# LSTM recurrence in rounds: low weights in pieces, another order between rounds, two-pass round with its rows in PSUM

## The reference

```python
x = x + gnn(layernorm(x), edge_index, W1, b1, W2, b2)     # segment sum over 100000 edges, two dense layers
x = x + ffn(layernorm(x)[None], W_f, b_f, ...)[0]
# ffn, for each of 6250 rows in order:
f_t = sigmoid(combined @ W_f + b_f); i_t = sigmoid(combined @ W_i + b_i)   # combined = (x_t, h_prev)
c_tilde = tanh(combined @ W_c + b_c)
c_t = f_t * c_prev + i_t * c_tilde
o_t = sigmoid(combined @ W_o + b_o)
h_t = o_t * tanh(c_t)
```

## Time and profile before

| | us |
|---|---|
| median of 3 runs | 2840.35 (2840.02 to 2848.08) |
| profiled execution | 2835.44 |
| its span, first to last instruction | 2833.9 |
| PE / DVE / ACT / POOL busy | 2506.7 / 2090.2 / 1585.3 / 1019.9 |

### The profile page before, as it was taken

How to read it: one execution, slowest core, us unless ns; L and a number is a source line. 1 busy time by engine, 2 the same in 40 slices (tenths; PEclk the granted TensorE clock), 3 DMA queues, 4 the chain that set the end, 5 groups by cost and what they waited for, 6 DMA issues and landing times.

```text
span 2833.9 us, 45183 instructions
## 1 busy us (share of the span) xinstructions
PE 2506.7 (88%) x10574; PEld 1840.8 (65%) x10575; DVE 2090.2 (74%) x5442; ACT 1585.3 (56%) x3682; POOL 1019.9 (36%) x1022
## 2 busy tenths in 40 slices
PE   6977999999999999998799988888887888788776
PEld 5765787788888778786566656666664555555444
DVE  5847888888888888887578766666666667666665
ACT  4644544454554444453267744444445888777775
POOL 0307777777777777776300000000000000033332
PEclk9998999999999999999899999999998999999998
DMA  8548988888898888887566557777776777689996
GB/s 238 154 137 249 281 265 259 250 272 271 269 280 270 253 254 265 249 265 227 171 166 185 147 168 237 235 234 231 236 237 170 212 204 213 187 233 260 270 266 188
DMA packets 209753, 648.73 MB, mean 229 GB/s; under 512 B 48762, under 2 KB 76794, under 8 KB 179954
## 3 DMA queue, kind: packets, MB, share of 16 engines
q1 hardware_dynamic: 136888, 410.93, 49.9%
q0 software_dynamic: 72816, 237.24, 28.3%
HBM read 493.87 MB, written 154.16 MB: 229 GB/s over the span
## 4 chain that ended last, share of the span: by engine, by line
PE 29%; DMA 6%; ACT 6%; DVE 6%; issue 2%; SPq 1%; DVEq 0%; ACTq 0%
PE acc L1506 24%; DMA xg<-total_rows 6%; PE hturn L1524 3%; ACT acc L1444 3%; ACT tc L1436 2%; ACT gate L1410 1%; DVE ic L1779 1%; PE acc L1532 1%; DVE total L1750 1%; DVE h L1792 1%; DVE c L1784 1%; DVE fc L1772 1%; DVE total L1752 1%; PE acc L1535 0%; DVE state L1766 0%
## 5 line engine op out<-in xcount | busy, mean ns | idle before, releaser
L1506 PE MATMUL acc<-W_high,state 128*125 128x512 f32 x2224 | 629.4, 417 | 71.6 <-ACT acc L1444 69.7
L1506 PEld LDWEIGHTS acc<-W_high,state 128*125 128x125 f32 x2224 | 410.4, 192 | 206.5 <-ACT acc L1444 88.2
L1359 POOL TENSOR_TENSOR out<-h,lx 125x512 f32<-125x512 f32 x50 | 64.3, 1286 | 1224.2 <-DVE h L1792 1224.2
L809 POOL DMA_INDIRECT rows<-ln_table,slab x400 | 400.7, 1002 | 249.5 <-issue 145.3
L809 POOL DMA_INDIRECT Wh<-ln_table,slab x400 | 430.4, 1076 | 121.9 <-issue 119.8
L910 PE MATMUL agg<-high,onehot 128*125 128x512 f32 x800 | 332.8, 416 | 29.7 <-DVE onehot L1007 18.5
L1506 PE MATMUL acc<-W_high,hT 128*125 128x512 f32 x784 | 325.1, 415 | 8.3 <-issue 0.2
L1020 DVE TENSOR_TENSOR low_part<-rows,high 128x512 fp32r<-128x512 f32 x400 | 254.1, 691 | 98.1 <-ACT high L866 83.5
L910 PE MATMUL agg<-low_part,onehot 128*125 128x512 f32 x800 | 322.0, 403 | 0.0
L1506 PE MATMUL acc<-W_low,hT 128*125 128x512 f32 x784 | 308.6, 394 | 0.0
L1772 DVE TENSOR_TENSOR fc<-gate,c 125x256 f32<-125x256 f32 x376 | 162.9, 433 | 188.6 <-ACT gate L1410 179.3
(11 more groups left out here) (211 smaller groups left out, 4483.1 us busy)
## 6 DMA issues: line engine op xcount, KB each, us to landing
xg<-total_rows SPq DMA_DIRECT2D x100, 896.0 KB
xg<-gate_rows SPq DMA_DIRECT2D x88, 896.0 KB
gate_rows<-gout SPq DMA_DIRECT2D x100, 448.0 KB
total_rows<-total SPq DMA_DIRECT2D x50, 896.0 KB
hT<-h_steps SPq DMA_DIRECT2D x98, 250.0 KB, 3.7
lx<-x_rows POOLq DMA_DIRECT2D x50, 250.0 KB, 8.6
out_dram<-out POOLq DMA_DIRECT2D x50, 250.0 KB, 8.7
h_steps<-hT SPq DMA_DIRECT2D x49, 250.0 KB, 3.2
```

Source lines behind the costliest of these rows:

```text
L809: e.indirect_dma_start(out=rows[j // 2][:, j % 2 * D:(j % 2 + 1) * D], out_offset=None, in_=table[:, :], in_offset=bass.IndirectOffsetOnAx ...
L1506: m = e.matmul(acc[n][0:L, :], stationary[:, k, :], weights[:, k, n // 2, n % 2].rearrange("p s c -> p (s c)"), start=begins, stop=(k == K ...
```

## The change

It edits `lstm_part` alone.

- Low weights: POOL makes them in 16 pieces of 512 columns, each behind the `decay` of a step of the rough round (the first behind that round's second step), and signals after every fourth.
- Near round: the rows of a step are copied into PSUM one step ahead (banks 0 and 3 by ACT, 1 and 2 by DVE), products add to them, gates are read from PSUM, and the sums are copied out to `total` (banks 0, 1, 2 by DVE, 3 by ACT) before the bank is seeded again. SP loads the rows of step s + 1 in step s. PE forms bank 3 of the first chunks after banks 0 and 1. At the first step PE adds the rows as fp32 products.
- Delta rounds: bank 0 gets its rows from PE (`add_rows(0)`), bank 3 from DVE, banks 1 and 2 from ACT as before.
- Between rounds: separate signals behind the transposes of `c`, of `decay` and of the gate; PE adds rows 0 and 1 before the start signal; the start signal comes after `state`, and a second one after `c`; what isn't needed for the start goes behind it. The near round's check is computed later: `h_gap` after the start of the delta round, its maxima in the measure and correct parts of the delta round, scaled by TOLERANCE / LOOSE, as two more columns of the last round's check.

```diff
@@ gpsimd @@
+            def low_weights():
+                for n in range(4 * K):
+                    k, half, bank = n // 4, n // 2 % 2, n % 2
...
+                    e.wait_ge(s_decay, AHEAD + LEFT_OUT + n + 2)
+                    piece = e.tensor_tensor(W_low[:, k, half, bank].rearrange("p s c -> p (s c)"),
...
@@ sync, near round @@
                     def keep(s, par, state_too):
-                        e.wait_ge(s_sum[3], f * STEPS + s + (AHEAD + 1))
+                        hold(e, s_passed, s_taken_out_v, s * 3 + 3)
+                        hold(e, s_passed, s_taken_out_a, s + 1)
                         spread(e, totals_v[s], total[par][0:L].rearrange("c a b g -> c (a b g)"), s_total_st[par])
...
@@ scalar @@
                     elif kind in DELTAS:
                         forget_input(1)
                         new_cell(FIRST)
                         cell_gate(1)
-                        seed(0)
                         seed(1)
                         output_gate(1)
                     elif kind == "near":
                         new_cell(FIRST)
+                        seed(0)
                         forget_input(1)
                         take_turned(FIRST, s, par, now)
                         cell_gate(1)
...
                     new_cell(SECOND)
                     if kind in DELTAS:
                         seed(2)
+                    elif kind == "near":
+                        take_out(3)
                         seed(3)
@@ tensor @@
                     def first_step():
-                        e.wait_ge(s_begin, r + 1)
-                        for n in range(4):
-                            m = add_rows(n)
-                        m.then_inc(s_taken, 1)
-                        for n in range(4):
+                        add_rows(0)
+                        add_rows(1)
+                        e.wait_ge(s_begin, r * 2 + 1)
+                        for n in range(2):
+                            for k in range(K):
+                                product(n, k)
+                        add_rows(2)
+                        e.wait_ge(s_begin, r * 2 + 2)
+                        add_rows(3).then_inc(s_taken, 1)
+                        for n in range(2, 4):
                             for k in range(K):
                                 product(n, k)
...
                     def delta_step():
+                        add_rows(0)
                         turn(FIRST, 1 - par, now - 1)
...
                     def near_step():
-                        for n in range(3):
-                            e.wait_ge(s_sum[n], summed - 1)
-                            products(n, FIRST, of_state, True)
+                        for n in range(2):
+                            seeded(n)
+                            add(n, FIRST)
+                        seeded(2)
+                        add(2, FIRST[:1])
                         if not first:
                             turn(SECOND, 1 - par, now - 1)
-                        e.wait_ge(s_sum[3], summed - 1)
-                        products(3, FIRST[:1], of_state, True)
+                        add(2, FIRST[1:])
                         for k in SECOND:
                             stated(k)
                         for n in range(2):
-                            products(n, SECOND, of_state, False).then_inc(s_acc[n], 1)
-                        products(3, FIRST[1:], of_state, False)
-                        products(2, SECOND, of_state, False).then_inc(s_acc[2], 1)
-                        products(3, SECOND[:1], of_state, False)
+                            add(n, SECOND).then_inc(s_acc[n], 1)
+                        seeded(3)
+                        add(3, FIRST).then_inc(s_taken, 1)
+                        add(2, SECOND).then_inc(s_acc[2], 1)
+                        add(3, SECOND[:1])
                         turn(FIRST, par, now)
@@ vector @@
+                    def take_out(n):
+                        half, bank = n // 2, n % 2
+                        e.wait_ge(s_total_st[par], (s - par) * (SPREAD // 2) + SPREAD)
+                        e.wait_ge(s_o[half] if bank else s_fi[half], now)
+                        e.tensor_copy(total[par][0:L, half, bank], acc[n][0:L, :]).then_inc(s_taken_out_v, 1)
+                    if kind == "near":
+                        forgotten(0)
+                        take_out(0)
+                        taken_in(0)
+                        for k in FIRST:
+                            new_cell(k)
+                        take_out(1)
+                        new_h(FIRST)
+                        seed(1)
+                        forgotten(1)
+                        take_out(2)
+                        seed(2)
+                        taken_in(1)
...
```

More of the change, by code:

```diff
@@ L1694, in measure @@
                 t.then_inc(s_ends, 1)
-                if kind not in ("rough", "delta"):
-                    e.wait_ge(s_worst, f + 1)
+                if kind in ("last", "more"):
+                    e.wait_ge(s_worst, f)
                     e.transpose(worst_t, worst[:, :], ident[:, :]).then_inc(s_worst_t, 1)
             def correct(r, kind):
+                if kind == "near":
+                    e.wait_ge(s_taken_out_a, STEPS)
                 e.wait_ge(s_cs, r + 1)
@@ L1825, in step @@
                             decayed()
-                        if kind == "rough" and not last:
-                            seed()
+                        seed(3)
                     else:
-                        if kind == "more" and not first:
+                        if not first:
                             low_part(SECOND, now - 1)
@@ L1851, in step @@
                         decayed()
-                        if kind == "more" and last:
+                        if last:
                             low_part(SECOND, now)
@@ L1885, in measure, with most_of @@
                     after_own(e.tensor_tensor(h_gap[:, k, 1:], hturn[k][:, 0:L - 1], h_start[:, k, 1:], ALU.subtract))
[L1886 to L1889 removed]
+            def most_of(n, g, op):
+                after_own(e.tensor_reduce(most[:, n:n + 1], g[:, :, :].rearrange("p k l -> p (k l)"), AX_X, op))
@@ new lines, in of_near_round, with measure @@
+            def of_near_round(n, op, sign):
+                most_of(n, h_gap, op)
+                after_own(e.tensor_scalar(most[:, n:n + 1], most[:, n:n + 1], sign * TOLERANCE / LOOSE, None, ALU.mult))
+            def measure(r, kind, f):
+                own[0] = own_before(r, kind)
+                signals[0] = 0
+                if kind == "delta":
+                    of_near_round(4, ALU.max, 1.0)
+                e.wait_ge(s_ends, r * 4 + 1)
+                after_own(e.tensor_tensor(gap[:, :, 1:], c_end_t[:, :, 0:L - 1], c_start[:, :, 1:], ALU.subtract))
+                if kind in ("rough", "near", "delta"):
+                    return
+                h_moved(r, kind)
+                for n, (g, op) in enumerate(((gap, ALU.max), (h_gap, ALU.max), (gap, ALU.min), (h_gap, ALU.min))):
+                    most_of(n, g, op)
@@ L1904, in correct @@
             def correct(r, kind):
+                e.wait_ge(s_ends, r * 4 + 2)
                 for k in range(K):
```

253 lines of the change are left out of this document (141 added, 112 removed).

## The result

The changed kernel takes 2816.97 us (median of 8 runs, 2802.63 to 2833.22) against 2841.59 for the kernel before (8 runs, 2838.65 to 2848.08): ratio 0.9916, 95% interval 0.9893 to 0.9939. The interval stands for 17 to 30 us less, so the times can't tell the 20 that I forecast from the 24.6 between the medians. I had forecast 2820, with a range of 2800 to 2833.

What follows compares the result with a forecast made beforehand. It took serial chains to bound the first three rounds and DMA bytes the last; terms -13.1 + 1.6 - 2 + 2.5 - 6.5 + 1 - 2.5 - 1 = -20 gave 2820 us, range 2800 to 2833.

Steps and rivals of the forecast that it cites:

- Start and pieces: Rough round: long POOL subtractions leave its start, -13.1 us; sixteen gated pieces cost +1.6 (bounds 0 and 7.8).
- The order of PE's first step: Start of rough round: PE forms banks 0 and 1 before adding rows 2 and 3, first gates earlier, -0.9 us.
- Rough to two-pass: Transition: `gap` 2.0 us earlier, cast and copy moved behind the start, fp32 additions added; -2 us (bounds 0 and -3.5).
- Two-pass steps: Additions leave the chain, copies and seeds join it; +0.05 us times 49, +2.5 (bounds -15 and +20).
- Two-pass to delta: Transition: check moved behind the start, rows added earlier, but row 0 lands late; -6.5 us (bounds -3 and -10).
- Delta steps: Delta round: PE's wait for ACT's seeds goes, transposes move 0.27 later, about cancelling; +1 us (bounds -3 and +7).
- Delta to last: Transition: products may begin earlier, but two additions stand among them; -2.5 us (bounds 0 and -4).
- Final check: End of kernel: `gap` earlier and one small operation less; -1 us.
- The forecast's case: Whole kernel: 2820 us, own range 2811 to 2830, chance 0.62.
- the start held back by late rows: Rival at the rough round's start: not freed because rows land late; 2824 us, counted inside the forecast's own range.
- The shorter two-pass step: Rival: both additions leave the chain and copies hide, -0.4 us a step, 2798 us; chance 0.15.
- the copies that take the chain: Rival in two-pass steps: copies and seeds lengthen the chain; +0.7 a step, 2852 us, chance 0.07; +0.4, 2837, chance 0.06.

Runs made afterwards that it cites:

- e1: Kernel before plus only the low weights in sixteen gated pieces on POOL, nothing else of the change; ratio 0.9962 to the kernel before, recurrence 1423.3 us against 1435.0.
- e6: Changed kernel with all sixteen pieces released after the first rough step instead of one a step; rough round 239.9 us against 225.9 in the changed kernel.
- e10: Changed kernel with 48 of the last round's 50 loads of x rows left out (output invalid); last stretch 322.2 us against 346.2.
- e4: Changed kernel with the two-pass round's seed of bank 2 moved from DVE to ACT; two-pass 466.1 us against 500.2, ratio 0.9805 to the kernel before.
- e7: Changed kernel with seed 2 and the copy out of bank 0 on ACT, delta row 0 loaded early; two-pass 456.3 us, ratio 0.9777 to the kernel before.
- e5: Changed kernel with the two-pass round's check put back ahead of the corrected state; turn-to-turn into delta 22.21 us against 22.87, recurrence 1411.6 us.
- e3: Changed kernel with the delta round's first row loaded in the last two-pass step, ahead of the stores; delta stretch 316.5 us against 324.0.

## Why the prediction was right, and where it was not

The sum was -20, the recurrence shows -21.5, and the medians -24.6, with the graph part's own variation in them. That the sum lies so near is in part luck: five terms missed by 2 to 3.4 us each, three one way and two the other, and the last stretch alone varies by 19 us from profile to profile. What held is where the gain would come from: the start and the places between rounds, and not the steps. Term by term:

- **Start and pieces, -13.1 + 1.6 = -11.5 forecast, -11.5 measured** (e1: -11.3). Its parts were off and cancelled. PE's start gave 1.8 and not 4.0. The two products held by the subtraction gave more than the 8.2 that I had: in e1, which has the pieces alone, the first gates of the first two steps stand 6.94 us apart, where it had been 15.66, -8.7, and the second step became 0.7 shorter too (5.65 for 6.32), which I had not counted. The order of PE's first step gave 0 and not 0.9 (above). The pieces cost 0 and not 1.6. For the start I had divided row 0's bytes by the whole bandwidth, while its load took 7.3 us with three more rows issued behind it. For the pieces, the rule in the Trainium skill, "SBUF — State Buffer", section "Who interferes with whom", which I had set beside the sum, was the better guide. By that rule in the Trainium skill, a copy with a single SBUF input outside the two-port modes doesn't hold a piece back. The trace agrees, with 0.69 and 1.29 side by side. That a product of two SBUF operands and a piece block each other whole is borne out by e6, with 1.52 for 0.42.
- **Rough to two-pass, -2 forecast, -4.3 measured** at the first gate (13.07 for 17.38). `gap`, and with it `c_start`, came 2.1 sooner as worked out, but the two additions took 2.2 us and lay beside the new states and the copy of `c`; I had them 3.1 long and on the path. The clock has a part in the rest: in e10, with the same code and a mean granted clock of 0.73 in place of 0.90, 2.6 of the 4.3 were left.
- **Two-pass steps, +2.5 forecast, -0.9 measured.** The balance held: what left the chain came back onto it. Two of its debits were measured by e4 and e7: 0.70 for the seed into bank 2 alone (I had 0.86 for it and the copy before it), 0.20 for the copy out of bank 0 (0.16). From the second `fc` to the second `h` it is 2.84 us, where it had been 1.52: 1.32 for those two copies, the whole 0.60 and 0.72 of my sum, with nothing of the 0.46 that I took off for a wait. So something else in the step gained more than I gave it; one such part is seen, the second transposes, which follow `h` by 0.35 us and not 0.79 (-0.44, I had -0.35). No run separates the rest, ACT's +0.42 among it, and that these errors cancelled is luck. The place where the time went is DVE's order in front of the second `ic`, as written; of PE's wait for `h` before its transposes, which I had left standing, 11.5 us of 49.2 are left.
- **Two-pass to delta, -6.5 forecast, -3.5 measured.** That PE would wait for the row was right, and its size was not: 6.68 us. I had the load issued at +5.2 us behind the last transposes (it was +5.5) and landed at +10.3 (it was +12.55), again by bytes over bandwidth plus one microsecond. The first product came 6.4 sooner, for 8. So -3.5 lay inside the bound of -3 only just. What I called DVE's gain was worth nothing there (e5).
- **Delta steps, +1 forecast, -1.2 measured** (301.1 for 302.3 from first to last transposes): nothing, 0.02 a step. PE's wait for ACT's seeds, 24.7 us over 46 steps, is gone, as forecast, but PE now waits 19.9 us over 45 steps for `state`: the wait has moved, and the step is as long. (The addition does take 0.86 us at full clock, up to the start of the next matmul; half of the 1.53 would be 0.77.)
- **Delta to last, -2.5 forecast, +0.6 measured,** which is 0 given how this stretch varies. The transition gave 5.4 and the round took it all. I had written that the last round goes by bytes, and still let half of the transition through.
- **Final check, -1 forecast, -0.6 measured.**

The forecast's case came in. Of the rivals, the start held back by late rows came in by half. The shorter two-pass step (-0.4 a step) and the copies that take the chain (+0.4 and +0.7) didn't, though the edits of e4 and e7 show how near the first one was: with two copies on ACT, where there was room, instead of ahead of DVE's products, the steps of the two-pass round take 443.1 us, 44.9 less than in the kernel before.

## What to carry to other kernels

When work is taken off a serial chain and copies are put in its stead, ask on which engine each copy stands and who is queued behind it: one 0.69 us copy in front of a product that others wait for cost 0.70 us in each of 49 steps, and nothing on an engine that was waiting there. A faster transition pays only if what it waits for next is there (here one load stood behind stores that it didn't need, 7.5 us) and only if the stage behind it isn't bound by bytes. And where an untouched part varies by more than the effect, compare stretches that begin behind it.

## What the runs showed of the hardware

- A row load of 1.02 MB took 6.6 to 7.3 us from issue to the matmul that waited for it, with other rows issued behind it; at the 251 GB/s of the earlier trace rows as many bytes move in 4.1.
- PE's additions ahead of the last round ran at half clock before and at full clock after. The windows say it (the granted clock is the third column from the right; before, then after):

```profile
2479.00:2484.50 5.50, 5.33 (x7) 2.33 (x8) 0.11 (x1) 0.00 (x0) 0.00 (x0) 0.53 0.69 183
```

```profile
2472.00:2474.00 2.00, 2.00 (x8) 0.78 (x7) 1.79 (x6) 0.16 (x1) 0.00 (x0) 1.00 1.04 267
```

0.53 is nearly all at the lower of the two levels (1.2 and 2.4 GHz), 1.00 is the upper. The eight slow records took 6.17 us, four fast ones 1.88. Ahead of the delta round, where PE now waits 6.68 us for the row, the clock is 0.50 when it goes on, and four records take 3.78. The idle time just in front doesn't settle the level, though. Before, PE had been idle 2.68 us in front of the additions and 3.28 shortly before that; after, 1.80, but e3 has 2.63 us at the same place and stays at 1.00:

```profile
2824.98 0.70 PE L1771 MATMUL acc<-ident,c_start 128*125 128x128 f32 x4 [2.63 <-DVE c_start L2001]
```

And in the changed kernel the clock was down just before, while PE ran its twelve transposes, from 2467.0 on, with 1.07 us of idle time in front of them:

```profile
2467.00:2470.30 3.30, 2.76 (x13) 2.37 (x12) 2.69 (x6) 0.00 (x0) 0.00 (x0) 0.50 1.06 230
```

So I give the levels as the clock of these executions, and no run here shows what sets them.
- The last round, with the same instructions, took 333 to 352 us (DMA share 0.97 and 0.96 in the shortest and the longest), and the graph part 1,754 to 1,810 us on three chips and 1,399 to 1,417 on the first, while the stages bound by the engines repeat within 3.0 us.
